# Moving the transposes of the normalised tile from TensorE to VectorE in a two-layer transformer kernel, with reordered queues and a last tile closed block by block

## What is computed

```python
x = x + attn0(ln(x))     # 16 heads, linear attention: phi(q) @ (phi(k).T @ v), phi = silu + 1
x = x + ffn0(ln(x))      # h = silu(x W1 s1) * (x W2 s2); h = gelu(h H1 s); h = gelu(h H2 s); h W3 s3
x = x + attn1(ln(x))     # one head, softmax(q k.T / 16) @ v, output projection
x = x + tanh(ln(x) @ weight @ aux1 @ aux2 + bias)
```

## Time and profile before

| | |
|---|---|
| median of 3 runs | 2042.87 us |
| the profiled execution | 2039.22 us |
| its span, first to last instruction | 2037.5 us |
| PE busy | 1988.6 us, 98% |
| DVE busy | 1237.9 us, 61% |
| ACT busy | 792.3 us, 39% |
| POOL busy | 379.5 us, 19% |
| mean granted PE clock | 0.994 |

### The profile page before, as it was taken

One profiled execution on the slowest core, in us unless ns is written; L12 is line 12 of the kernel. 1 busy time (PEld: TensorE's weight loads), 2 busy tenths in 40 slices (PEclk: granted clock), 3 DMA queues, 4 the chain that ended last, 5 costly groups with the idle time before them and its releaser, 6 DMA issues.

```text
span 2037.5 us, 37348 instructions
## 1 busy us (share of the span) xinstructions
PE 1988.6 (98%) x15484; PEld 1918.9 (94%) x15484; DVE 1237.9 (61%) x2881; ACT 792.3 (39%) x1502; POOL 379.5 (19%) x347
## 2 busy tenths in 40 slices
PE   5999999999999999999999999999999999999996
PEld 4999999999999999999999999999999999999985
DVE  5645666566575656666466675656666566664465
ACT  2334335253443434435253343434335353342332
POOL 2011211122121121210222121121210212111111
PEclk8999999999999999999999999999999999999999
DMA  9600000000000000000000000000000000000000
GB/s 348 219 4 1 22 1 1 22 1 22 1 22 1 1 22 1 22 1 1 22 1 22 1 15 7 1 22 1 22 1 1 22 2 11 1 8 5 1 1 21
DMA packets 24453, 46.01 MB, mean 23 GB/s; under 512 B 1184, under 2 KB 21408, under 8 KB 24096
## 3 DMA queue, kind: packets, MB, share of 16 engines
q1 hardware_dynamic: 24272, 43.41, 6.1%
HBM read 35.02 MB, written 19.92 MB: 27 GB/s over the span
## 4 chain that ended last, share of the span: by engine, by line
PE 91%; DVE 5%; issue 2%; POOL 1%; ACT 0%; DMA 0%; POOLq 0%; DVEq 0%; ACTq 0%
PE ffn_fill L981 47%; PE att_fill L931 26%; PE ffn_fill L931 9%; PE ffn_fill L1039 6%; PE att_fill L999 1%; PE att_fill L1116 1%; DVE st L630 1%; DVE xn L643 1%; POOL rstd_C L599 1%; PE ffn_fill L1007 1%; DVE whole L697 1%; DVE x L715 0%; DVE xn_b L712 0%; DVE mv_C L634 0%; DVE late_xn L643 0%
## 5 line engine op out<-in xcount | busy, mean ns | idle before, releaser
L981 PE MATMUL ffn_fill<-act_hi,h 128*128 128x256 f32 x4096 | 986.4, 283 | 0.2
L981 PE MATMUL ffn_fill<-act_lo,h 128*128 128x256 f32 x4096 | 979.4, 281 | 0.0
L981 PEld LDWEIGHTS ffn_fill<-act_lo,h 128*128 128x128 f32 x4096 | 772.2, 189 | 4.8
L981 PEld LDWEIGHTS ffn_fill<-act_hi,h 128*128 128x128 f32 x4096 | 771.4, 188 | 5.4 <-POOL act_lo L613 0.8
L869 ACT ACTIVATE whole<-ffn_fill,scales 128x256 f32<-128x256 f32 x512 | 213.0, 472 | 429.1 <-PE ffn_fill L981 428.1
L706 DVE CAST act_hi<-whole 128x512 fp32r<-128x512 f32 x256 | 108.4, 424 | 270.8 <-ACT whole L869 269.2
L931 PE MATMUL ffn_fill<-half_hi,w 128*128 128x256 f32 x1024 | 254.0, 288 | 9.1 <-DVE whole L697 4.5
L931 PE MATMUL ffn_fill<-half_lo,w 128*128 128x256 f32 x1024 | 249.6, 283 | 0.0
L613 POOL TENSOR_TENSOR act_lo<-whole,act_hi 128x512 fp32r<-128x512 f32 x128 | 169.9, 1332 | 295.6 <-DVE act_hi L702 295.1
L931 PEld LDWEIGHTS ffn_fill<-half_hi,w 128*128 128x128 f32 x1024 | 195.5, 191 | 13.2 <-DVE whole L697 7.6
L931 PEld LDWEIGHTS ffn_fill<-half_lo,w 128*128 128x128 f32 x1024 | 196.2, 192 | 0.6
(11 more groups left out here) (218 smaller groups left out, 3270.4 us busy)
## 6 DMA issues: line engine op xcount, KB each, us to landing
x<-in_L_attn_x SPq DMA_DIRECT2D x16, 512.0 KB, 3.6
out<-x SPq DMA_DIRECT2D x16, 512.0 KB, 3.0
h<-scratch_h1T SPq DMA_DIRECT2D x2, 2048.0 KB, 10.5
h<-scratch_h2T SPq DMA_DIRECT2D x2, 2048.0 KB, 11.4
w<-scratch_w1T SPq DMA_DIRECT2D x1, 1024.0 KB, 9.5
w<-scratch_w2T SPq DMA_DIRECT2D x1, 1024.0 KB, 10.5
w<-scratch_w3T SPq DMA_DIRECT2D x1, 1024.0 KB, 26.2
rows<-in_rows SPq DMA_DIRECT2D x1, 640.0 KB, 5.9
```

The costliest lines, as they stand in the source:

```text
L981: last = pe.matmul(two(bank)[:, o, :], view(w), view(moving[:, k, :]), start=k == 0 and o == 0 and half == 0, stop=k == KH - 1 and half == ...
```

## The change

1. **T in BODY.** The eight PE transposes go. DVE transposes `xn` in 32x32 blocks into a new view `turned` (which shares the memory of `qz_lo`): 16 instructions, each on 32 partitions and 256 elements of them. ACT copies `turned` to `xt_hi`; the subtraction for `xt_lo` goes to POOL. The steps of PROLOGUE, FIRST and END keep the old form under the name LT (in END also for the last tile's attention).
2. **Orders.** All BODY orders are written anew. PE runs U0 to G3a without a break, then c:CV and c:CZ.
3. **CF** uses two banks of 512 columns instead of four of 256.
4. **END**: the last tile's closing steps DST, DNO, T, CF are cut into ES, EN, ET, EF for each of the four 128-token blocks, with their own buffers, and each block is stored by its own DMA.
5. **PROLOGUE and FIRST**: 24 PE transposes without use (WARM24) at the start and four before BT0; the first FOLD becomes FA0 to FA2 in PROLOGUE, in the ring `ffn_fill`, and TAKE becomes TA0 to TA2; the attention weights are split in two steps (PREP0, PREP1) that wait for two DMAs each. The weights for FOLD are loaded ahead of the ternary matrices, and H1 and H2 are bounced through scratch and loaded in halves.

```diff
+SQ = 32
-    "T": {"att_fill": 2, "xt_hi_ready": 2},
+    "T": {"turned": 1, "xt_hi_ready": 2, "xt_lo_ready": 2},
-    "CF": {"att_fill": 4, "tanh_done": 4, "out_ready": 1},
+    "CF": {"att_fill": 2, "tanh_done": 2, "out_ready": 1},
 PE_ORDERS BODY
-    U0 U1 U2 U3a c:T U3b G0a c:CV c:CZ G0b G1a c:CS0 G1b G2 c:CP0 c:CS1 G3a c:CS2 G3b c:CO0 c:CP1 H0a c:CS3
-    H0b c:CO1 c:CP2 H1a c:CO2 c:CP3 H1b H2 c:CO3 H3 BT1 W0 U0a c:T U0b U1 c:CF a:T U2 U3a a:AKV0 a:AKV1
-    a:AKV2 a:AKV3 U3b G0a a:AS a:AQa G0b a:AQb G1 G2 a:AM G3 a:AOa H0 a:AOb H1 H2 H3 n:BT0 W1
+    U0 U1 U2 U3 G0 G1 G2 G3a c:CV c:CZ G3b c:CS0 H0 c:CP0 c:CS1 c:CS2 c:CO0 c:CP1 c:CS3 c:CO1 c:CP2 H1a
+    c:CO2 c:CP3 H1b H2a c:CO3 H2b H3 BT1 W0 U0 U1 U2 U3a c:CFa U3b G0a c:CFb G0b G1 G2 G3 a:AKV0 a:AKV1
+    a:AKV2 a:AKV3 H0 H1a a:AS a:AQ a:AM H1b H2a a:AO H2b H3 n:BT0 W1
 DVE_ORDERS BODY
+    c:CSTa U0 U1 c:CSTb U2 U3 c:CNO c:T G0 G1 c:CQ c:CV c:CZ G2 c:CS0 G3 c:CP0 c:CS1 c:CS2 c:CO0 c:CP1 c:CS3
+    c:CO1 c:CP2 H0 c:CO2 BST1 c:CP3 BNO1 a:AST c:CO3 c:DST H1 H2 c:DNO c:Ta H3 BT1 c:Tb W0 U0 U1 U2 U3 a:ANO
+    c:CF a:T G0 G1 G2 a:AKV0 a:AKV1 G3 a:AKV2 a:AKV3 a:AS a:AQ a:AM H0 a:AO n:BST0 n:BNO0 H1 H2 H3 n:BT0 W1
 POOL_ORDERS BODY
+    U0 U1 c:CST U2 U3 c:T c:CB BST1 a:AST c:DST c:T U0 U1 U2 U3 c:CF a:T a:AB n:BST0
...
 (DVE)
+                elif kind == "T":
+                    norm = "ANO" if who == "a" else "DNO" if ("DNO", 0, who == "d") in c.seen else "CNO"
+                    dve.wait_ge(s[own.own + "xn_ready"],
+                                c.value(own.own + "xn_ready", c.ago(own.own + "xn_ready", norm, 0, who == "d") + NB))
+                    wait(dve, s["xt_lo_ready"], c.value("xt_lo_ready"))
+                    for there in range(P // 2 if share == "b" else 0, P // 2 if share == "a" else P, SQ):
+                        for here in range(0, P, SQ):
+                            into = turned[there:there + SQ].rearrange("p k (b n) -> p b k n", b=NB)
+                            last = dve.transpose(into[:, :, :, here:here + SQ],
+                                                 own.xn[here:here + SQ].rearrange("p b (k n) -> p b k n", k=KD)
+                                                 [:, :, :, there:there + SQ])
+                    if share != "a":
+                        last.then_inc(s["turned"], 1)
 (ACT)
+                elif kind == "T":
+                    act.wait_ge(s["turned"], c.value("turned", 1))
+                    for k in range(KD):
+                        act.activation(own.xt[0][:, k, :], turned[:, k, :], ACT.Copy)\
+                           .then_inc(s[own.own + "xt_hi_ready"], 1)
 (POOL)
+                elif kind == "T":
+                    for k in range(KD):
+                        wait_apart(pool, s[own.own + "xt_hi_ready"], c.value(own.own + "xt_hi_ready", k + 1))
+                        pool.tensor_tensor(own.xt[1][:, k, :], turned[:, k, :], own.xt[0][:, k, :].bitcast(F32),
+                                           ALU.subtract).then_inc(s["xt_lo_ready"], 1)
 END, last block of d: on DVE
+    d:CP3 d:EN2 c:CF d:CO3 d:ET2 d:EF2 d:ES3 d:EN3 d:ET3 d:EF3
 PE_ORDERS PROLOGUE
+    WARM24 a:LT a:AKV0 a:AKV1 a:AKV2 a:AKV3 f:FA0 a:AS a:AQ a:AM a:AO f:FA1 f:FA2 WARM4 n:BT0 CHECK0
 DVE_ORDERS PROLOGUE
+    a:AST a:ANO PREP0 a:LT a:AKV0 SCALE a:AKV1 a:AKV2 a:AKV3 PREP1 a:AS f:TA0 a:AQ a:AM LOOK00 LOOK01 a:AO
+    n:BST0 f:TA1 n:BNO0 f:TA2 CHECK0 n:BT0
```

More of the change, by code:

```diff
@@ L198, in copy @@
         return other
-STAGE_OF = {"AST": "A", "BST": "B", "CST": "C", "DST": "C"}
+STAGE_OF = {"AST": "A", "BST": "B", "CST": "C", "DST": "C", "ES": "E"}
 def stage_of(step):
@@ L214 @@
 PROLOGUE = steps_from("""
-    a:AST a:ANO a:AB PREP a:T a:AKV0 SCALE a:AKV1 a:AKV2 a:AKV3 a:AS a:AQ a:AM LOOK00 a:AO
-    n:BST0 LOOK01 n:BNO0 n:BT0 CHECK0""")
+    WARM24 a:AST a:ANO a:AB PREP0 a:LT a:AKV0 SCALE a:AKV1 a:AKV2 a:AKV3 PREP1 a:AS f:FA0 a:AQ f:FA1 a:AM f:FA2 LOOK00 LOOK01
+    f:TA0 a:AO f:TA1 n:BST0 f:TA2 n:BNO0 WARM4 n:BT0 CHECK0""")
 FIRST = steps_from("""
-    U0 a:AST U1 a:ANO U2 a:T U3 LOOK10 a:AB a:AKV0 a:AKV1 LOOK11 a:AKV2 LOOK12 a:AKV3 LOOK13 CHECK1 a:AS a:AQ
-    G0 a:AM FOLD0 G1 TAKE0 a:AO WIDE G2 LOOK20 LOOK21 FOLD1 TAKE1 G3 LOOK22 LOOK23 CHECK2 LOOK30
+    U0 a:AST U1 a:ANO U2 a:LT U3 LOOK10 a:AB a:AKV0 a:AKV1 LOOK11 a:AKV2 LOOK12 a:AKV3 LOOK13 CHECK1 a:AS a:AQ
+    G0 a:AM G1 a:AO WIDE G2 LOOK20 LOOK21 FOLD0 TAKE0 G3 LOOK22 LOOK23 CHECK2 LOOK30
     H0 CHECK3 H1 BST1 BNO1 H2 H3 BT1 W0 U0 U1 U2 U3 G0 G1 G2 G3 H0 H1 n:BST0 n:BNO0 H2 H3 n:BT0 W1""")
@@ L222 @@
 END = steps_from("""
[L223 to L226, removed]
+    U0 U1 U2 U3 G0 G1 G2 G3 H0 H1 BST1 BNO1 H2 H3 BT1 W0 U0 U1 U2 U3 G0 G1 G2 G3 H0 H1 c:CST c:CNO H2 c:LT H3 c:CB W1
+    d:CST c:CQ c:CV c:CZ d:CNO d:LT c:CS0 c:CS1 d:CB d:CQ d:CV c:CP0 c:CO0 d:CZ c:CP1 c:CO1 c:CS2 c:CS3
+    d:CS0 d:CS1 c:CP2 c:CO2 c:CP3 c:CO3 d:CP0 d:CO0 c:DST d:CS2 d:CP1 d:ES0 d:CO1 d:EN0 c:DNO d:CS3 d:ET0 c:LT d:ES1 d:EN1
+    d:CP2 d:EF0 c:CF d:CO2 d:ET1 d:EF1 d:ES2 d:CP3 d:EN2 d:CO3 d:ET2 d:EF2 d:ES3 d:EN3 d:ET3 d:EF3""")
 def order_from(plan):
@@ L234 @@
 PE_ORDERS = {
+    "PROLOGUE": order_from("""
+    WARM24 a:LT a:AKV0 a:AKV1 a:AKV2 a:AKV3 f:FA0 a:AS a:AQ a:AM a:AO f:FA1 f:FA2 WARM4 n:BT0 CHECK0"""),
     "FIRST": order_from("""
-    U0 U1 a:T U2a a:AKV0 a:AKV1 a:AKV2 U2b a:AKV3 U3 CHECK1 a:AS a:AQ a:AM FOLD0 G0a a:AOa G0b a:AOb G1 G2
-    FOLD1 CHECK2 G3 H0 H1 H2a CHECK3 H2b H3 BT1 W0 U0 U1 U2 U3 G0 G1 G2 G3 H0 H1 H2 H3 n:BT0 W1"""),
+    U0 U1 U2a a:LT U2b U3a a:AKV0 a:AKV1 a:AKV2 a:AKV3 U3b CHECK1 a:AS a:AQ G0a a:AM G0b G1a a:AO G1b G2a
@@ L246 @@
+    c:CS0 c:CS1 d:CV c:CP0 d:CZa c:CO0 c:CP1 d:CZb c:CO1 c:CS2 d:CS0 c:CS3 d:CS1 c:CP2 d:CP0 c:CO2 c:CP3
+    d:CO0 d:CS2 c:CO3 d:CP1 d:CO1 d:CS3 d:ET0 d:CP2 d:EF0 c:LT d:CO2 d:ET1 c:CFa d:EF1 d:CP3 c:CFb d:CO3
+    d:ET2 d:EF2 d:ET3 d:EF3"""),
 }
 DVE_ORDERS = {
+    "PROLOGUE": order_from("""
+    a:AST a:ANO PREP0 a:LT a:AKV0 SCALE a:AKV1 a:AKV2 a:AKV3 PREP1 a:AS f:TA0 a:AQ a:AM LOOK00 LOOK01 a:AO
+    n:BST0 f:TA1 n:BNO0 f:TA2 CHECK0 n:BT0"""),
     "FIRST": order_from("""
-    a:AST U0 a:ANO U1 a:T LOOK10 LOOK11 a:AKV0 a:AKV1 a:AKV2 LOOK12 LOOK13 a:AKV3 U2 CHECK1 a:AS U3 a:AQ
@@ L254 @@
-    c:CP2 c:CO2 BST1 H0 c:CP3 H1 BNO1 a:AST c:CO3 H2 c:DST H3 BT1 c:DNO W0 c:T a:ANO c:CF U0 a:T U1 a:AKV0
-    a:AKV1 a:AKV2 a:AKV3 U2 U3 a:AS G0 a:AQ a:AM G1 G2 G3 a:AO n:BST0 n:BNO0 H0 H1 H2 H3 n:BT0 W1"""),
+    c:CSTa U0 U1 c:CSTb U2 U3 c:CNO c:T G0 G1 c:CQ c:CV c:CZ G2 c:CS0 G3 c:CP0 c:CS1 c:CS2 c:CO0 c:CP1 c:CS3
+    c:CO1 c:CP2 H0 c:CO2 BST1 c:CP3 BNO1 a:AST c:CO3 c:DST H1 H2 c:DNO c:Ta H3 BT1 c:Tb W0 U0 U1 U2 U3 a:ANO
+    c:CF a:T G0 G1 G2 a:AKV0 a:AKV1 G3 a:AKV2 a:AKV3 a:AS a:AQ a:AM H0 a:AO n:BST0 n:BNO0 H1 H2 H3 n:BT0 W1"""),
@@ L256 @@
     "END": order_from("""
[L257 to L260, removed]
+    U0 U1 U2 U3 G0 G1 G2 G3 H0 H1 BST1 BNO1 H2 H3 BT1 W0 U0 U1 U2 U3 G0 c:CST G1 G2 G3 H0 c:CNO H1 H2 c:LT
@@ L261 @@
+    c:CQ H3 W1 d:CST c:CV d:CNO c:CZ d:LT c:CS0 c:CS1 d:CQ c:CP0 c:CO0 c:CP1 d:CV d:CZ c:CO1 c:CS2 d:CS0
+    c:CS3 d:CS1 c:CP2 d:CP0 c:CO2 c:CP3 d:CO0 d:CS2 c:CO3 d:CP1 d:ES0 c:DST d:CO1 d:EN0 d:CS3 c:DNO d:ET0
+    d:ES1 d:EN1 d:CP2 d:EF0 c:LT d:CO2 d:ET1 d:EF1 d:ES2 d:CP3 d:EN2 c:CF d:CO3 d:ET2 d:EF2 d:ES3 d:EN3
+    d:ET3 d:EF3"""),
 }
 ACT_ORDERS = {
+    "PROLOGUE": order_from("""
+    PREP0 a:LT a:AKV0 a:AKV1 a:AKV2 a:AKV3 PREP1 a:AQ a:AM LOOK00 LOOK01 n:BT0"""),
     "FIRST": order_from("""
-    U0 U1 a:T LOOK10 a:AKV0 a:AKV1 a:AKV2 LOOK11 LOOK12 a:AKV3 U2 LOOK13 a:AQ a:AM U3 LOOK20 LOOK21 G0 G1
+    U0 U1 a:LT a:AKV0 LOOK10 U2 a:AKV1 a:AKV2 a:AKV3 LOOK11 LOOK12 U3 LOOK13 a:AQ LOOK20 a:AM G0 G1 LOOK21
@@ L273 @@
 }
 POOL_ORDERS = {
+    "PROLOGUE": order_from("""
+    a:AST a:AB n:BST0"""),
     "FIRST": order_from("""
@@ L277 @@
     "BODY": order_from("""
-    c:CST U0 U1 c:CB U2 U3 BST1 a:AST c:DST U0 c:CF U1 a:AB U2 U3 n:BST0"""),
+    U0 U1 c:CST U2 U3 c:T c:CB BST1 a:AST c:DST c:T U0 U1 U2 U3 c:CF a:T a:AB n:BST0"""),
     "END": order_from("""
-    U0 U1 U2 U3 BST1 U0 U1 U2 U3 c:CST d:CST c:CB d:CB c:DST d:DST c:CF d:CF"""),
+    U0 U1 U2 U3 BST1 U0 U1 U2 U3 c:CST d:CST d:CB c:CB d:ES0 c:DST d:ES1 d:EF0 d:EF1 d:ES2 c:CF d:EF2 d:ES3
+    d:EF3"""),
 }
@@ L804, in part, with take_split @@
                            .then_inc(wide, 1)
-                elif kind == "TAKE":
-                    first = c.ago("att_fill", "FOLD", j)
-                    def take_split(k, dst, nth):
-                        bank, out = filled(dve, c, "att_fill", first + k)
+                elif kind in ("TA", "TAKE"):
+                    def take_split(ring, k, dst, nth):
+                        bank, out = filled(dve, c, ring, k)
                         dve.tensor_copy(dst[0][:], two(bank)).then_inc(s["fold_hi"], 1)
@@ L956, in ffn_products, with wait_turned @@
                     emit(lambda ap: ap)
+            def wait_turned(c, own, who):
+                if ("T", 0, False) in c.seen and who != "d":
```

(7 more changed lines are left out.)

284 lines of the change are left out of this document (178 added, 106 removed).

## The result

The changed kernel takes 2081.07 us (median of 4 runs, 2080.29 to 2082.28) against 2040.78 us for the kernel before (4 runs, 2037.11 to 2043.28): ratio 1.0198, 95% interval 1.0186 to 1.0211. Forecast were 2005 us and a range of 1980 to 2050; neither held. The profiled execution took 2082.28 us with a span of 2080.5.

The account below looks back on a forecast made before the run. PE, busy 98% of the span, was taken as the bound. From 2039.2 us, 23.4 for 14 turns, 8 at the start and 4 at the end gave 2003.8, for the median 2005; range 1980 to 2050.

Parts of the forecast that it names:

- What leaves PE: PE in a BODY turn: without its transposes 3.5 us less, 0.88 for a T, floor of a turn 119.4 us.
- What DVE gets: DVE in BODY: 16 transposes per T at 0.33 us, 5.3 in all; 0.44 and 7.0 if each waits, by the quadrant rule.
- Place 3: From the last softmax block to the next half: DVE needs 13.9 us against PE's 12.7, so PE waits 1.2.
- Place 1: Before c:CV: `xt_lo` ready at 19.3 us, PE there at 20.8; hidden, 0.3 put down for POOL colliding with DVE.
- Place 2: G0 directly behind U3: the last pair of U passes ACT, DVE and POOL with nothing between, 0.3 us.
- Second half: a:T between CF and G0: T, ACT and POOL take 9 us, PE has 13 before AKV0, so hidden.
- Start: PROLOGUE and FIRST: waits for the clock and FOLD's matmuls go, 8 us less, between 3 and 11.
- both terms for the clock: At the start, AKV and U0 no longer at half clock: 2.8 and 2.4 us less.
- End: From the end of CO3 on PE to the kernel's end, last tile cut by blocks: 4 us less, 0 to 8.
- each transpose waits for the last: Rival, 20%: T 7.0 to 7.4 us, turn 123.4 to 123.8, time 2034 to 2041, PE's gain given back as waits.
- DVE becomes the bound, slower than before: Rival, 15%: a transpose costs 0.5 us or more, 2061 at 0.5; slower than before from 0.45 each.
- Granted clock 1.0 in U0: Sign that the forecast holds: PE's granted clock stays at 1.0 during U0.

Follow-up runs that it names:

- e9: New edges, in BODY only a:T on DVE and POOL, and CFa moved on PE to between U1 and U2: 2017.86 us, 0.989 of the kernel before.
- e2: The changed kernel with each DVE transpose reading the 32-partition quadrant it writes, so not a true transpose: 2040.91 us, 1.0008 of the kernel before.
- e3: The changed kernel with 8 of the 16 transposes per T, ACT and POOL reading xn instead of turned: 2010.07 us, 0.9856 of the kernel before.
- e8: The changed kernel with POOL subtracting only 16 of 512 columns in each subtraction for `xt_lo`: 2054.88 us, 1.0074 of the kernel before.
- e4: The changed kernel with DVE doing H3 and BT1 before the whole second c:T, not between its halves: 2100.74 us, 1.0297 of the kernel before.
- e7: The changed kernel with only its second c:T back on PE and CF in four banks: 2041.24 us, 1.0 of the kernel before.
- e1: The changed kernel with BODY as before the change, only PROLOGUE, FIRST, END and loads new: 2028.93 us, 0.9945 of the kernel before.
- e6: New edges, in BODY only a:T on DVE and POOL, and FIRST's steps that wait for H1 placed later: 2027.51 us, 0.994 of the kernel before.

## Why the prediction was wrong

Point by point, in its own steps:

- **What leaves PE** was right: 0.88 for a T (e9 gains 0.85), and a floor of 119.5 against 119.4. The same subtraction gives 119.5 in e2 and e3 too.
- **What DVE gets** failed first. "I take 0.33": measured 0.45 where the quadrant changes, as the alternative of 0.44 said. T = 7.2. The `bn_stats` that I went by all start on partition 0. They show overlap within a quadrant, and e2's 0.33 to 0.37 confirms them for that; they said nothing on the case at hand. The condition in which the rule and my row differ was named, and I took the row that could not test it. DVE's load in a turn came to 99.6 us, not 88.5; with POOL's subtractions cut short (e8) it is 94.5.
- **Place 3**, "PE waits 1.2 us": measured 4.39 in W0 and before the banks of U1 and U2. Its own sum with T = 7.2 gives 8.6 + 7.2 - 12.7 = 3.1, so 1.9 of the miss is T. The last 1.3: U2's bank, 0.76, which waits for a step behind `x<-x,xn_b`, lengthened by POOL (e8); two slow first matmuls of 0.11; and 0.3 that I put down to handovers, which no run separates.
- **Place 1**, "0.3": 1.35. All of it goes in e2 and e3 (shorter T) and in e8 (no long subtraction); it takes both. "Collisions of POOL with DVE's two-input steps behind T" named the right engines at a fifth of the price; a part of the price, 1.2 us on DVE, lies ahead of T, in the cast and CNO.
- **Place 2**, "0.3": 0.80, the same in the changed kernel, e2, e3, e4, e7 and e8. The 0.39 at c:CO1 was not foreseen, and these kernels have it alike: between c:CP1 and c:CO1 PE has only c:CS3, where the old order had a part of H0 on either side of it, and DVE's low part comes 0.3 us too late. These 1.2 us of a turn, some 17 in all, belong to the new orders and not to T on DVE. No run has the new orders with all T on PE.
- **Second half** hidden: right. No wait at a:AKV0, and e9 runs a:T (7.17 us on DVE) with none.
- **Start**, "-8": -3.1. AKV at half clock got only shorter (8.4 us to 7.0 in e1), and U0 at half clock did not go (0.21 between starts for most of it): both terms for the clock were too large. The new loads let H1 land late. Chain of waits of e1:

```profile
40.78 16.93 DMA h<-scratch_h1T
...
59.14 1.49 DVE lowsum L928
```

  PE waits 4.0 us for that `lowsum`. How much the load order alone costs was not tried; e6 shows that moving the steps on DVE does not heal it.
- **End**, "-4": -6.8.

A turn was forecast at 121.2 and is 126.45. The 5.25 between them: place 3 3.2, place 1 1.05, place 2 0.5, c:CO1 0.4, floor 0.1. Over 14 turns 73.5 us. With the miss at the edges (7.0 gained instead of 12; 5.0) that is 78.5, and the profiled execution missed 2003.8 by 78.5. Alone (e1) the edges are worth 9.8; of the 2.8 us that are missing beside the new BODY, 0.9 lie behind the last c:CV (68.0 us to the end, 67.1 in e1), and the rest is open.

How much is the transposes' spacing? e2 takes away 2.8 of the turn. e8 takes away 2.1 by POOL. They must not be added: the 1.35 before c:CV is in both. The forecast would have been wrong with overlapping transposes too: e2 stands at no change. Of the rivals, "each transpose waits for the last" has the mechanism, but its turn of 123.4 to 123.8 lacked some 2.8 us; "DVE becomes the bound, slower than before" has the sign. Its point of decision, 0.45 for each, was met exactly, and its price at that point, no change, was not. "Granted clock 1.0 in U0" did not hold in five turns, at little cost (e4).
